# Convolution stage of a hybrid block: four batches one after another, or as one pipeline with its loads

## The reference, cut to what matters

```python
# L0: one-channel maps over all pixels, then a gated residual
theta, phi, g = (einsum('bchw,oc->bohw', x, w) + bias  for each)     # one channel each, N = 1024 pixels
y  = theta * (sum_j phi_j * g_j) / N
s  = x + batch_norm(y * w_w + w_b)                                   # per channel, running statistics
gate = sigmoid(relu(mean_hw(s) @ fc1.T) @ fc2.T)
x  = s * gate
# L1: block attention on the group norm of x (32 groups of 8 channels); blocks of 2 x 2, windows of 4 x 4
x  = x + L1(group_norm(x)) 
```

## Time and profile before

| | us |
|---|---|
| median of three runs (4584.33 to 4596.33) | 4592.86 |
| the profiled execution | 4597.95 |
| its span, first to last instruction | 4596.1 |
| PE, DVE, ACT, GpSimd busy in the span | 3815.5, 2885.5, 2027.1, 909.8 |
| start of the first map, of the first dot product | 22.33, 37.17 |
| end of the last addition of the convolution stage | 193.67 |

### The profile page before, as it was taken

The page is one execution under the profiler, slowest core; times in us unless marked ns, Lnnn a source line. Parts: engine busy times, 40 slices in busy tenths (PEclk is TensorE's granted clock), DMA queues, the critical chain, the costliest instruction groups (busy, mean ns, idle before and its releaser), DMA issues. The chain is left out here.

```text
span 4596.1 us, 171603 instructions
## 1 busy us (share of the span) xinstructions
PE 3815.5 (83%) x71052; PEld 2272.9 (49%) x71053; DVE 2885.5 (63%) x6291; ACT 2027.1 (44%) x4155; POOL 909.8 (20%) x2309
## 2 busy tenths in 40 slices
PE   3469999789799986688898669999999999875995
PEld 1236666434366663345555434445444444444763
DVE  3547777400477774578888548858858858843343
ACT  1123344221334341466666427747747747611221
POOL 0001111000011110355555201111111211105022
PEclk7679999899799997899999779999999999977997
DMA  1000000000000000100000000000000000034223
GB/s 49 0 10 0 0 0 0 4 18 0 8 0 0 0 0 4 44 1 1 1 1 1 0 11 1 0 1 0 0 1 0 0 1 0 1 117 168 66 90 102
DMA packets 47250, 80.84 MB, mean 18 GB/s; under 512 B 7120, under 2 KB 38128, under 8 KB 46064
## 3 DMA queue, kind: packets, MB, share of 16 engines
q1 hardware_dynamic: 40944, 61.84, 3.9%
q0 software_dynamic: 6144, 16.79, 1.1%
HBM read 45.05 MB, written 33.55 MB: 17 GB/s over the span
## 5 line engine op out<-in xcount | busy, mean ns | idle before, releaser
L1680 PE MATMUL psum<-hm_ex,hm_mix 128*128 128x512 f32 x1024 | 510.9, 622 | 42.1 <-ACT hm_Aq L1760 38.1
L1746 ACT ACTIVATE hm_ex<-psum,hm_nm 128x1024 f32<-128x1024 f32 x256 | 285.6, 1116 | 298.4 <-DVE hm_nm L1804 298.4
L1680 PEld LDWEIGHTS psum<-hm_ex,hm_mix 128*128 128x128 f32 x1024 | 175.8, 191 | 352.6 <-issue 344.9
L1819 DVE COPY hm_A<-psum 128x1024 f32<-128x1024 f32 x256 | 313.0, 1222 | 51.2 <-PE psum L1689 47.8
L1814 DVE TENSOR_SCALAR_CACHE_REDUCE hm_plus<-hm_Aq,hm_cbcol,hm_sums 128x1024 f32<-128x1024 f32 x256 | 340.6, 1330 | 0.0
L1804 DVE TENSOR_REDUCE hm_nm<-psum 128x1 f32<-128x1024 f32 x256 | 311.1, 1215 | 14.1 <-PE psum L1668 14.1
L670 PE MATMUL psum<-fw_w,fw_stage 128*128 (+1 forms) x512 | 247.3, 568 | 76.7 <-DVE fw_vh L844 51.7
L1689 PEld LDWEIGHTS psum<-K,hm_Aq 128*128 128x128 f32 x2048 | 236.7, 140 | 149.9 <-issue 145.2
L1751 ACT ACTIVATE hm_junk<-hm_Aq 128x1024 f32<-128x1024 f32 x256 | 270.6, 1057 | 30.3
L1668 PE MATMUL psum<-hm_kt,hm_qd 64*32 64x512 f32 x4096 | 280.5, 606 | 0.0
L1226 ACT ACTIVATE pt_signs<-pt_acts,pt_tb 128x1024 f32<-128x1024 f32 (+1 forms) x224 | 227.5, 1018 | 115.4 <-POOL pt_tb L1093 94.7
(11 more groups left out here) (358 smaller groups left out, 8003.2 us busy)
## 6 DMA issues: line engine op xcount, KB each, us to landing
ex_rows_in<-ex_zero SPq DMA_DIRECT2D x2, 5120.0 KB, 25.3
ex_xs<-ex_rows_in SPq DMA_DIRECT2D x80, 128.0 KB, 2.0
ex_rows_out<-ex_ys SPq DMA_DIRECT2D x80, 128.0 KB, 1.7
ex_w<-in_ex_w SPq DMA_DIRECT2D x2, 4096.0 KB, 22.7
X<-in_x SPq DMA_DIRECT2D x2, 2048.0 KB, 10.8
out_y<-X SPq DMA_DIRECT2D x2, 2048.0 KB, 9.0
ff_w<-in_ff_w SPq DMA_DIRECT2D x2, 1024.0 KB, 5.8
pt_w_proc<-in_pt_proc SPq DMA_DIRECT2D x1, 2048.0 KB, 7.6
```

What stands on the lines that cost most here:

```text
L1680: mm = pe.matmul(bank[4 + c], mix[:, u, :], ex[:, u, 512 * c:512 * c + 512], start=True, stop=True)
L1746: act.activation(ex[:, u, :], flat2(psum[:, 2 * u:2 * u + 2, :]), ACT.Exp, bias=nm[:, u:u + 1], accum_out=rsum[:, u:u + 1]).then_inc(s_ex, 1)
L1819: dve.tensor_copy(A[:, :, :, QT_ * t:QT_ * t + QT_], flat2(psum[:, 6:8, :]).rearrange("p (m g n) -> p m g n", m=MT, g=HEADS)).then_inc(s_a ...
```

## The change

`load_stage` is gone; its loads are issued in `conv_stage`, X batch by batch, with a semaphore each (s_x), and the others in three groups (s_rep, s_small, s_wide). The loops over batches are written out. In the list of each engine:

- SP issues c_rep, c_rep_b, X of batch 0, V, c_fc1, c_fc2, K, X of batch 1, c_wv, c_wo, X of batches 2 and 3.
- PE computes the maps of batch b + 1 between the small products of batch b. A bank may be written again when the dot product has read it (s_dot). The products with wv and wo are now made batch by batch (`windows`, 196 columns), one or two batches behind, in bank 7, which fc2's output shares.
- ACT copies a half of the maps as soon as its g and theta are there (`maps_out`), loads the two tables ahead of time by a dummy activation (`load_table`), copies the window products (`windows_out`) and adds bo to X of the batches 0 to 2. The root of bn_var now follows the copies of batch 0.
- GpSimd, idle in this stage before, does the window sums of channel half 1 for batches 0 to 2 and the additions of c_om for batches 0 to 2.
- DVE does the window sums of half 0 one batch later, between the pooled mean and the gate; for batch 3 both halves, bo and the additions. Scale and shift (c_gv) have two buffers. The sums' scratch exists twice, for DVE and GpSimd.

```diff
 def conv_stage(k):
+                load_x = lambda b: sp.dma_start(
+                    X[:, :, wide(b)], d["x"][b].rearrange("(h p) n -> p h n", p=P)).then_inc(s_x[b], 16)
...
             def _(pe):
-                pe.wait_ge(s_w, 96)
-                with pe.Fori(0, B) as b:
-
-                    pe.wait_ge(s_img, b + 1)
+                def maps(b, n, q):
+                    if b >= B:
+                        return
+                    if b:
+                        pe.wait_ge(s_dot, 2 * b - 1 + n)
...
+                def windows(b):
+                    pe.wait_ge(s_pg0, b + 1)
+                    if b < B - 1:
+                        pe.wait_ge(s_pg1, b + 1)
+                    pe.wait_ge(s_exp, min(b + 2, B))
+                    if b:
+                        pe.wait_ge(s_om, b)
...
+                for b in range(B):
+                    if b + 1 < B:
+                        pe.wait_ge(s_x[b + 1], 16)
+                    maps(b + 1, 0, 0)
                     pe.wait_ge(s_pool, b + 1)
...
+                    maps(b + 1, 0, 2)
+                    maps(b + 1, 0, 1)
+                    maps(b + 1, 1, 0)
+                    maps(b + 1, 1, 2)
+                    if b == B - 1:
+                        windows(b - 1)
                     pe.wait_ge(s_gst, b + 1)
...
+                    maps(b + 1, 1, 1)
+                    if b == 0:
+                        pe.wait_ge(s_wide, 32)
+                    elif b < B - 1:
+                        windows(b - 1)
+                windows(B - 1)
...
             def _(act):
+                for n in range(2):
+                    maps_out(0, n)
                 act.wait_ge(s_var, 1)
                 act.activation(inv[:, 1, :], inv[:, 0, :], ACT.Sqrt).then_inc(s_std, 1)
...
+            @block.gpsimd
+            def _(pool):
+                own = Steps(pool, s_pch)
+                for b in range(B):
+                    pool.wait_ge(s_gv, b + 1)
+                    if b < B - 1:
+                        window_sums(own, pool, 1, b, 1).then_inc(s_pg1, 1)
+                    if b:
+                        pool.wait_ge(s_bo, b)
+                        pool.wait_ge(s_om, b)
+                        for h in range(CH):
+                            for r in range(2):
+                                own.mark(spread_add(pool, b - 1, h, r))
+                own.sync()
...
             def _(dve):
...
                     dve.tensor_tensor(pooled[:, :], pooled[:, :], inv[:, 3, :], ALU.add).then_inc(s_pool, 1)
+                    if b:
+                        window_sums(own, dve, 0, b - 1, 0).then_inc(s_pg0, 1)
                     dve.wait_ge(s_exp, b + 1)
...
+                    if b > 1:
+                        dve.wait_ge(s_pg1, b - 1)
...
-                dve.wait_ge(s_om, 4)
+                dve.wait_ge(s_gv, B)
+                own.done(window_sums(own, dve, 0, B - 1, 1))
+                window_sums(own, dve, 0, B - 1, 0).then_inc(s_pg0, 1)
```

More of the change, by code:

```diff
@@ L113, in load_stage @@
 @stage
-def load_stage(k):
-    nc, d = k.nc, k.d
-    s = k.sem("s_loaded")
-    with nc.Block() as block:
-        @block.sync
-        def _(sp):
-            sp.dma_start(k.K[:, :, :], d["const"]).then_inc(s, 16)
-            sp.dma_start(k.V[:, :, :], d["vec"]).then_inc(s, 16)
-            for h in range(CH):
-                sp.dma_start(k.X[:, h, :].rearrange("p (b n) -> p b n", b=B),
-                             d["x"][:, P * h:P * h + P, :].rearrange("b p n -> p b n")).then_inc(s, 16)
-            sp.wait_ge(s, 16 * (2 + CH))
-@stage
 def conv_stage(k):
@@ L203, in _ @@
+                pe.wait_ge(s_rep, 32)
+                pe.wait_ge(s_x[0], 16)
+                for n in range(2):
+                    for q in (0, 2, 1):
+                        maps(0, n, q)
+                pe.wait_ge(s_small, 64)
+                for b in range(B):
+                    if b + 1 < B:
+                        pe.wait_ge(s_x[b + 1], 16)
+                    maps(b + 1, 0, 0)
                     pe.wait_ge(s_pool, b + 1)
                     for h in range(CH):
-                        mm = pe.matmul(bank[6][0:R, 0:1], fc1[:, h, :], pooled[:, h:h + 1],
+                        mm = pe.matmul(small[0:R, 0:1], fc1[:, h, :], pooled[:, h:h + 1],
@@ L248, in _ @@
[L248 to L254 removed]
+                    k.load_table(act, ACT.Sqrt)
@@ new lines, in _ @@
+                    if b + 1 < B:
+                        maps_out(b + 1, 0)
+                    else:
+                        windows_out(b - 1)
+                    act.wait_ge(s_gvar, b + 1)
+                    act.activation(v[:, 2, :], v[:, 1, :], ACT.Sqrt).then_inc(s_gsd, 1)
+                    if b + 1 < B:
+                        maps_out(b + 1, 1)
+                    if b and b < B - 1:
+                        windows_out(b - 1)
+                    if b:
+                        act.wait_ge(s_pg0, b)
+                        act.wait_ge(s_pg1, b)
+                        for h in range(CH):
+                            last = act.activation(X[:, h, wide(b - 1)], X[:, h, wide(b - 1)], ACT.Identity,
+                                                  bias=k.vec("bo", h))
+                        last.then_inc(s_bo, 1)
@@ L333, in _ @@
-                last.then_inc(s_dch, 1)
-                dve.wait_ge(s_dch, own.n + 1)
+                    own.done(dve.tensor_copy(gr[:, :], small[:, 0:2 * CH]))
+                    if b > 1:
+                        dve.wait_ge(s_pg1, b - 1)
+                    own.done(dve.tensor_tensor(v[:, 0, :], gr[:, 0:CH], gr[:, 0:CH], ALU.mult))
+                    own.done(dve.tensor_tensor(v[:, 0, :], gr[:, CH:2 * CH], v[:, 0, :], ALU.subtract))
+                    dve.tensor_scalar(v[:, 1, :], v[:, 0, :], EPS, None, ALU.add).then_inc(s_gvar, 1)
@@ new lines, in _ @@
+                window_sums(own, dve, 0, B - 1, 0).then_inc(s_pg0, 1)
+                dve.wait_ge(s_pg0, B)
+                for h in range(CH):
+                    own.done(dve.tensor_scalar(X[:, h, wide(B - 1)], X[:, h, wide(B - 1)], k.vec("bo", h), None,
+                                               ALU.add))
+                dve.wait_ge(s_om, B)
+                for h in range(CH):
+                    for r in range(2):
+                        own.mark(spread_add(dve, B - 1, h, r))
+                own.sync()
@@ L2304, in program @@
         k = Core(nc, ctx, d)
-        load_stage(k)
         conv_stage(k)
```

185 lines of the change are left out of this document (95 added, 90 removed).

## The result

The changed kernel took **4511.23 us** (median of four runs, 4510.56 to 4513.94) beside 4590.82 for the kernel before (now of four runs): a ratio of **0.9828**, with a 95% interval of [0.9811, 0.9845]. Timed once more, later, it gave 4512.63 and 0.9829 [0.9815, 0.9843]; there one run of the kernel before, 5254.83 us at a granted clock of 0.72, is left out as slow. The forecast was 4509, range 4492 to 4535. So the number held. The terms behind it did not all hold, and that is what the rest is about.

What follows compares the result with a forecast made beforehand. The prediction took the stage to be bound by latency, its engines taking turns. Savings of 15.6 + 0 + 53.8 + 14.2 = 83.6 us gave 4509 us against the median, range 4492 to 4535.

Steps and rivals of the forecast that it cites:

- GpSimd's hindrance: Batches: delay of VectorE's steps by GpSimd working beside them, priced at nothing in the forecast sum.
- the chain: Batches: VectorE's steps from first dot to the group norm's scale, without stalls 16.2 us in batch 0, 16.7 from batch 1.
- ScalarE's stall: Batches 2 and 3: gate late behind ScalarE's window copies and additions of bo, 1.3 us each.
- Part 1, the loads: Start of the stage: first map at 6.7 us instead of 22.33, saving 15.6 us.
- Part 2, the first batch: First map to first dot: earlier copying and the later root cancel, net 0 within half a us.
- the root's 2.9: First batch: table load, root of bn_var and small VectorE steps, now behind the copies, delay the first dot 2.9 us.
- Part 3, the batches: The four batches: 74.5 us instead of 128.25, stalls included, saving 53.8 us.
- The rival that carried it: Batches: GpSimd holds VectorE up by its share of two-operand steps, 8.9 us, giving 4518 us; chance 0.2.
- TensorE's stall: Batches: group mean's average queued behind four maps of the next batch, 2.2 us in batch 0, then 1.7 twice.
- Part 4, the tail: After the batches: only batch 3's work is left, 14.0 us instead of 28.25, saving 14.2 us.
- The clock that never rises: Rival, maps and windows: TensorE stays at the low clock, +34 us, giving 4543 us; chance 0.1.
- the slow GpSimd: Rival, batches: GpSimd becomes the bound at 5 us an instruction, +22 us, giving 4615 us; chance 0.01.

Runs made afterwards that it cites:

- Experiment 4: Changed kernel with TensorE waiting for all four loads of X before its first map: first map at 19.27 us, next stage starts 11.5 us later.
- experiment 3: Changed kernel with the root of bn_var ahead of batch 0's copies on ScalarE's queue again: next stage starts 2.7 us earlier.
- experiment 1: Changed kernel without GpSimd's window sums and output-map additions: stretch from second dot to next stage 9.1 us shorter; whole time 8872 us, as a later search was executed.
- experiment 10: Changed kernel with root first, second map ahead of the gate, additions beside the statistics, and GpSimd's sums moved too: 4496.88 us, ratio 0.9797 to the kernel before.
- experiment 2: Changed kernel with GpSimd's additions waiting until VectorE finished the next batch's window sums: next stage's first product at 116.72 us, against 116.16.

## Why the prediction was right, and which of its steps were not

- **The sum** was 83.6 us, the stage gave 78.7, the medians 79.6. Terms that were off in opposite directions are behind this closeness, so it is partly luck. In the batches GpSimd's hindrance, priced at nothing, added 8.1 us, while the chain came out 3.6 shorter than forecast, ScalarE's stall 2.6 and TensorE's 1.3: together +0.6, 75.1 for 74.5.
- **Part 1, the loads: right in kind, 1.5 us too high** (first map at 6.7; measured 8.20, and 8.4 to 9.0 in later profiles). The rate was right: until 6.0 us 224 GB/s, 1.34 MB, had moved, as reckoned. The term that failed is "with the way to PE I take 6.7", 0.7 us for which no row was named. PE began 2.2 us later, when by the stretch above, 264 GB/s over 8.20 us, 2.16 MB had moved, so 0.7 MB of loads issued behind batch 0 went ahead of its landing. Whether the last pieces of batch 0 came late beside them, or the notice that all had landed, the views do not show. The loads did not share the rate evenly, which would have meant 13.5. Experiment 4 shows that this part counts in full.
- **Part 2, the first batch: held.** 15.2 measured, 14.8 forecast; experiment 3 takes the root's 2.9 out and gets 3.0.
- **Part 3, the batches: 53.8 forecast, 53.2 measured, from wrong parts.** "So I price DVE's delay at nothing, the nearest row" was the step that failed. GpSimd lengthened VectorE's steps by 10.2 us, 2.1 of them in the tail, and removing its work took 9.1 us off the stage, 1.3 of it the tail's product at a higher clock (experiment 1). The rival that carried it gave 8.9 by VectorE's share of two-operand steps: the mechanism was right there and the size near, and it should have stood in the sum. Which steps would pay it had only in part: the scaling of X, on its list, was never met, and two steps on one and two numbers per partition (L351, L352), not on it, paid 2.5 us. The row I had chosen against it was too thin for this: VectorE's step met the last 0.13 us of one GpSimd copy.
- **What made up for it.** The chain without stalls was shorter than the 16.2 and 16.7 of the forecast: 16.87 − 1.9 = 15.0 in batch 0, where the gate came 0.7 sooner than before (1.43 against 2.14), and 19.57 − 2.4 − 1.3 = 15.9 in batch 1. Over four batches 75.1 less 8.1 of hindrance and 4.3 of TensorE's stalls leaves 62.7 us in place of 66.3 (16.2 and three times 16.7). And ScalarE's stall of 1.3 in batches 2 and 3 did not show: VectorE's sums, 2.1 us longer, covered it. It came out as soon as they were short (1.13 and 1.54 in experiment 1). TensorE's stall came as forecast in batch 0 (1.9 for 2.2) and a little larger in batch 1 (2.4 for 1.7), and not at all in batch 2, where the clock stayed at 1.00 (the four maps took 8.8, 9.7 and 7.1 us, 9.0 forecast) and VectorE asked 2.1 us later. So three delays lay on top of one another, and pricing each alone would have been too much.
- **Part 4, the tail: 14.0 forecast, 16.5 measured.** VectorE's sums there were 2.1 longer, again beside GpSimd's additions, which the forecast had put "under the windows"; and the second product took 2.98 and not 2.4, since the clock stayed at 0.50 to the end.
- **The other rivals.** The clock that never rises and the slow GpSimd did not come: the batches ran at 0.86, and GpSimd's nine steps took 8.9 us of a batch of 19, for 8 forecast.

## What to carry to other kernels

When work goes to GpSimd, ask step by step what VectorE does at that time. In this kernel steps with two operands in SBUF, and scalings of SBUF data, paid for it. The dots, with one operand in PSUM, and the batch statistics did not: moving the additions beside the statistics gave 5.7 us, moving them behind the sums 0.75, no more than the scatter. When a trace has no clear row of a collision, take an estimate of it into the sum instead of nothing: here the rival's 8.9 us, for 10.2 measured. And when delays of three queues meet at the same engine, removing one shows the next: the root's place, the order on TensorE and GpSimd's timing gave 2.7, at most 1.35 and 5.7 us one by one, and 14 to 16 together.

## What the runs showed of the hardware

- A wait between GpSimd and VectorE is seen as a longer instruction, not as idle time: a VectorE step on one number per partition took 0.63 us in place of 0.16 and ended 0.02 us after GpSimd's. The loser changes: GpSimd's L166 took 1.35 us beside VectorE's L355, and the same step 0.50 beside the dots (experiment 10).
- Which VectorE steps pay was not by length or by operand count alone. Beside GpSimd's additions the scaling of X with one tensor operand took 2.39 us in place of 1.66 for a pair and the gate's first step 0.84 in place of 0.16 (experiment 2). The reciprocal right behind the gate's step stayed at 0.17. The statistics stayed at 694 ns and the dots, one operand in PSUM, at 0.75 in all runs. The Trainium skill (SBUF — State Buffer, section Who interferes with whom) names both kinds that paid, operations with two SBUF inputs, and `tensor_scalar`, the kind of the scalings, where its operands meet the conditions of a two-port mode. The runs agree on who paid (0.63 for 0.16, 2.39 for 1.66); in which mode a step ran they do not show.
- ScalarE's passes over 1024 columns of SBUF (L308) took 1132 to 1140 ns each beside GpSimd's work, and 1132 to 1139 with GpSimd idle (experiment 1).
- The clock made results jump: the same window product took 1.59 or 2.98 us in two profiles of one kernel, and 16 map steps 7.13 or 9.83 in two kernels that differ in GpSimd's waits alone, where the clock fell before those waits ended.
